# A four-stage transformer kernel on one core: Sinkhorn reciprocals in PSUM, other PSUM pairs for M, mix and attention tiles, whole-row subtractions on GpSimd

## The chip, the core and the metric

The kernel runs on one core of a Trainium2 chip. The metric is the device time of one execution, in microseconds (us); lower is better. The engines are named as in the profile: PE is the matmul engine (TensorE), DVE is VectorE, ACT is ScalarE, POOL is GpSimd, SP issues the DMAs. SBUF is the working memory of 128 partitions. PSUM is the accumulator memory: PE writes it, and DVE and ACT read and write it. This kernel uses it as four pairs of banks, PAIR[0] to PAIR[3], each 128 x 1024 f32.

## The reference, cut to what matters

Four blocks are applied to x (2 x 512 rows of 1024), each with a layer norm in front and a residual added behind:

```python
x = x + fake_quant(ln(x)) @ fake_quant(ctx)                    # 1: quantised product
x = x + hyper_connection(ln(x))                                # 2: Sinkhorn mixing of 4 streams
x = x + attention(ln(x), ctx, Wq, bq, Wk, bk)                  # 3: softmax(Q K^T / 32) @ ctx
x = x + lora_ffn(ln(x), gate, up, down)                        # 4: silu(gate) * up, hidden 2752
```

Block 2 needs, for every row, a 4 x 4 matrix that is normalised 50 times by rows and by columns:

```python
for _ in range(50):
    u = -logsumexp(Z + v[None, :], axis=-1)
    v = -logsumexp(Z + u[:, None], axis=-2)
H_res = exp(Z + u[:, None] + v[None, :])
x_mixed = einsum("tij,tjc->tic", (1 - g) * I + g * H_res, x_streams)
```

## The kernel before

Everything is scheduled by hand: each engine has one program in a fixed order, and engines meet in semaphores. The 1024 rows are eight tiles g = 0..7 of 128 rows; tiles 0 to 3 are batch 0, tiles 4 to 7 batch 1. Matmuls are done in f16 with a high and a low part, so that each product is three matmuls of 128 x 512 (`mm3`, L1894 to L1896). The lower parts are formed by subtracting the high part from the f32 value, on DVE, on ACT or on POOL.

**Sinkhorn.** DVE keeps the 4 x 4 matrices in linear form in SBUF. One step (`sinkhorn_step`, L1285) is three instructions, each waiting for the one before: a sum (L1290), a reciprocal (L1291, into RR, which lies in SBUF) and a product (L1292) of the matrix with the reciprocal, repeated over rows or columns. There are 99 steps for each batch. The first 30 (`JOINT`) are done for both batches at once, on 128 x 128 elements; then the matrices are copied apart (L1300) and 69 steps run on batch 0 alone (128 x 64 elements). The other batch's 69 steps (`second_steps`) come later, in pieces of 1, 27, 11, 11, 11, 6 and 2 between other DVE work: after each of the first pieces DVE takes the lower parts of two projected tiles (`projected_lo`, L1373), then the first score maximum (`maximum`, L1386).

**What runs beside the first Sinkhorn.** PE computes M = Wq^T Wk in eight tiles of two halves (`m_half`), each followed by the subtraction of its high part (`m_rest`, L2061), while ACT takes the high and the low part out of PSUM (L677, L681). M tiles go through three pairs in turn. Between them PE and ACT compute the branch product of block 2 through PAIR[3], and POOL adds its streams (L513 to L516) and adds the result to X (`add_share`, L521).

**After the first Sinkhorn.** `mix_factors` (L1311) gives the factors. Tiles 0 and 1 are mixed by DVE (L1338) and ACT (`mix_help`, L743). For tiles 2 and 3 ACT makes diagonal matrices (`mix_diag`, L755) and PE multiplies (`mix_product`, L2091) into PAIR[0] and PAIR[2]. Tiles 0 to 3 are then normalised (L760), transposed on PE (`third_transpose`, L2108), reduced by their high parts (`third_rest`, L2116) and projected (`project(0, n)`, n = 0..3, one call being 96 matmuls into one pair of PAIR[0] and PAIR[1]). The scores (`score(g)`) and attended tiles (`attend(g)`) follow in the same two pairs, managed by the class `Banks`; a second `Banks` object, `aux`, hands PAIR[2] and PAIR[3] in turn to the constant product, the transposed softmax weights (`weights_transpose`, L1976, read by ACT L821 and DVE L1398) and later transposes.

**The second Sinkhorn** runs on DVE beside `project(0, n)` and `score(0)`; it ends with `mix_factors(1)`, after which DVE mixes tiles 4 to 7 alone. Beside it POOL adds the shares of tiles 4 to 7 and takes the lower parts of context rows (`context_lo`, L531; DVE has its own, L1381). POOL does each row of 1024 in four instructions of 256. A context row's lower part also releases its staging slot to the next DMA.

The order of PE's program around the change is:

```python
mix_product(2); mix_product(3); m_rest(KD - 1)
for g in range(0, BT, 2):
    third_transpose(g); third_transpose(g + 1); third_rest(g); third_rest(g + 1)
```

Of the kernel before, what the change touches and what calls it, by code (L numbers as in the profile page):

```python
# [99 lines left out]
class Banks:  # L100
# [3 lines left out]
    def __init__(self, pairs, uses):  # L104
        self.pairs = pairs
        self.uses = uses
        self.place = {use[0]: i for i, use in enumerate(uses)}

    def pair(self, *name):
        return self.pairs[self.place[name] % len(self.pairs)]  # L110

    def wait_empty(self, eng, *name):
        before = self.place[name] - len(self.pairs)
        if before >= 0:
            eng.wait_ge(self.uses[before][1], self.uses[before][2])


def build(nc, x, ctx, ctx_t, consts, small_w, w_branch, wq, wk, bqk, gate_w, gate_tail, up_w,
          up_tail, down_w, down_tail, gate_a, gate_bt, up_a, up_bt, down_a, down_bt, out_t, x_keep):
    stack = ExitStack()  # L120
    with stack:
# [98 lines left out]
        MIX_PAIR = (None, None, 0, 2)  # L220
# [23 lines left out]
        def factors_of(g, si, sj):  # L244
# [72 lines left out]
            [(("ctk", 0), ctk_ok, 1)]  # L317
            + [(("at", g), at_lo, g + 1) for g in range(BT)]
# [14 lines left out]
        M_PAIR = (2, 1, 0, 2, 1, 0, 2, 1)  # L333
        T3_PAIR = (1, 3, 0, 2)
# [141 lines left out]
        def _(e):  # L476
# [47 lines left out]
            def context_lo(i):  # L524
                n, kind, b, k = context_item(i)
                tile = (CN if kind else CTT)[b][k]
# [3 lines left out]
                for q in range(0, D, CST):  # L530
                    last = e.tensor_tensor(tile[:, 1, q:q + CST], STAGE[n % SLOTS][:, q:q + CST], tile[:, 0, q:q + CST],  # L531
                                           ALU.subtract)
                last.then_inc(c_lo, 1)
# [630 lines left out]
        def _(e):  # L1164
# [119 lines left out]

            def sinkhorn_step(n, z, rs, rr):  # L1285
# [8 lines left out]
            def part(b):  # L1294

                return ZE[:, b * NE:(b + 1) * NE], RS[:, b * n32 // B:(b + 1) * n32 // B], RR[:, b * n32 // B:(b + 1) * n32 // B]
# [357 lines left out]
            for n in range(JOINT):  # L1654
                sinkhorn_step(n, ZP, RS, RR)
# [235 lines left out]
        def _(e):  # L1891
# [132 lines left out]
            def m_half(i, h):  # L2024

                if i == 0 and h == 0:
                    e.wait_ge(w_lo, 2 * KD)
                    e.wait_ge(ht_ok, 7)
                elif i == 1 and h == 0:
                    e.wait_ge(ht_ok, 8)  # L2030
                elif i == 2 and h == 0:
                    e.wait_ge(ctx_ok, 1)
                elif h == 0:
                    e.wait_ge(m_lo, i - 2)
# [49 lines left out]
            def mix_product(g):  # L2084

                dst = PAIR[MIX_PAIR[g]]
                e.wait_ge(m_lo, KD - 4 + g)
# [8 lines left out]
            def third_transpose(g):  # L2096
                e.wait_ge(n3_ok, g + 1)
                if g == 0:
                    e.wait_ge(m_lo, KD)
                elif g == 1:  # L2100
                    e.wait_ge(y_ok, NT)
                    e.wait_ge(braw_ok, 1)
                if g >= BT:
# [62 lines left out]
            def weights_transpose(g):  # L2166
                e.wait_ge(e_ok, g + 1)
# [199 lines left out]
            mix_product(2)  # L2367
            mix_product(3)
            m_rest(KD - 1)
# [137 lines left out]
```

## Time and profile before

| | |
|---|---|
| median of three runs | 1239.46 us (1236.49 to 1240.28) |
| the profiled execution | 1237.51 us, its span 1235.7 us |
| PE busy | 1169.7 us, 95% of the span |
| DVE busy | 797.1 us, 65% |
| ACT busy | 479.5 us, 39% |
| POOL busy | 128.9 us, 10% |

The profile is of one execution. The page gives busy time per engine, the span in 40 slices, and the chain of work that ended last. Other views list who waited for whom, busy time and granted PE clock in chosen stretches, and single instructions in order of time. PE's clock is given as a share of 2.4 GHz, so 0.50 is 1.2 GHz. A DVE instruction's duration includes whatever it waits for after it has started.

### The profile page before, as it was taken

To read this page: it belongs to the slowest core of one execution; us is meant where nothing else is said; L and a number is where in the kernel's file an instruction comes from. 1 tells how busy PE (TensorE), PEld (TensorE's weight loads), DVE (VectorE), ACT (ScalarE), POOL (GpSimd) and SP (SyncE) were. 2 spreads that over 40 slices of the span, in tenths; PEclk is the share of its full clock that TensorE was granted. 3 is DMA by queue.
4 is the path that set the end of the run, shared out by engine and by line. 5 is a ranking of instruction groups with operands and counts; after the bars stand their busy time and mean duration, and the time that the engine had idled before them with its cause. 6 is when DMAs were issued, how large, how long until landed. Compare 5 with 4: busy or idle time off the path is not lost.

```text
span 1235.7 us, 16385 instructions
## 1 busy us (share of the span) xinstructions
PE 1169.7 (95%) x6357; PEld 579.0 (47%) x6362; DVE 797.1 (65%) x1571; ACT 479.5 (39%) x716; POOL 128.9 (10%) x176
## 2 busy tenths in 40 slices
PE   3899999689999999999999999999999999999998
PEld 2345554454444445454444444444444444444444
DVE  6695898989997156887776776767767652222220
ACT  7782851574135124534434434334343231111110
POOL 4410260028002210020000000000001000000000
PEclk9989999899999999999999999999999999999999
DMA  9530000015012114220121121111111231111310
GB/s 370 208 115 1 1 1 1 0 69 152 19 36 100 49 35 139 69 101 24 46 69 68 36 69 44 59 69 34 69 52 24 71 136 46 46 47 46 119 38 26
DMA packets 26062, 83.58 MB, mean 68 GB/s; under 512 B 3648, under 2 KB 4288, under 8 KB 25984
## 3 DMA queue, kind: packets, MB, share of 16 engines
q1 hardware_dynamic: 25984, 82.53, 19.6%
q8 instruction: 51, 0.84, 0.3%
q14 instruction: 27, 0.22, 0.1%
HBM read 76.22 MB, written 6.29 MB: 67 GB/s over the span
## 4 chain that ended last, share of the span: by engine, by line
PE 75%; DVE 17%; ACT 5%; issue 2%; DMA 1%; ACTq 0%; SPq 0%; DVEq 0%
PE PAIR L2257 31%; PE PAIR L1894 11%; PE PAIR L1895 11%; PE PAIR L1896 11%; DVE LORA L1292 3%; DVE LORA L1291 3%; DVE LORA L1290 3%; DVE X L1338 2%; PE PAIR L1959 2%; PE PAIR L2214 2%; PE PAIR L1976 1%; PE PAIR L2091 1%; PE PAIR L1967 1%; PE PAIR L2269 1%; ACT POOL L617 1%
## 5 line engine op out<-in xcount | busy, mean ns | idle before, releaser
L1894 PE MATMUL PAIR<-POOL 128*128 128x512 f16 x688 | 261.3, 380 | 4.8 <-DVE POOL L1381 2.8
L1896 PE MATMUL PAIR<-POOL 128*128 128x512 f16 x688 | 261.3, 380 | 0.0
L1895 PE MATMUL PAIR<-POOL 128*128 128x512 f16 x688 | 261.3, 380 | 0.0
L2257 PE MATMUL PAIR<-XT,POOL 128*128 128x512 f16 (+1 forms) x1056 | 239.0, 379 | 1.0 <-ACT ST L867 1.0
L2257 PEld LDWEIGHTS PAIR<-XT,POOL 128*128 128x128 f16 (+1 forms) x1056 | 102.6, 98 | 120.5 <-issue 2.5
L2257 PE MATMUL PAIR<-X,POOL 128*128 128x512 f16 (+1 forms) x528 | 121.2, 379 | 0.0
L1896 PEld LDWEIGHTS PAIR<-POOL 128*128 128x128 f16 x688 | 67.2, 98 | 81.8 <-issue 0.6
L1894 PEld LDWEIGHTS PAIR<-POOL 128*128 128x128 f16 x688 | 67.1, 98 | 76.6 <-issue 5.5
L1895 PEld LDWEIGHTS PAIR<-POOL 128*128 128x128 f16 x688 | 67.2, 98 | 64.5 <-issue 0.8
L1509 DVE SCALAR_TENSOR_TENSOR STG<-STG,PAIR 128x1024 f32<-128x1024 f32 (+2 forms) x32 | 28.1, 884 | 92.1 <-PE PAIR L2269 89.1
L901 ACT ACTIVATE POOL<-STG 128x1024 f16<-128x1024 f32 (+2 forms) x32 | 25.0, 788 | 144.9 <-DVE STG L1509 144.9
L2257 PEld LDWEIGHTS PAIR<-X,POOL 128*128 128x128 f16 (+1 forms) x528 | 50.9, 98 | 57.4 <-issue 0.4
L1456 DVE TENSOR_TENSOR POOL<-STG,POOL 128x512 f16<-128x512 f32 (+1 forms) x110 | 72.3, 692 | 0.9 <-ACT POOL L852 0.7
L1292 DVE SCALAR_TENSOR_TENSOR LORA<-LORA 128x64 f32<-128x64 f32 (+1 forms) x168 | 61.3, 365 | 5.8
L852 ACT ACTIVATE POOL<-STG 128x512 f16<-128x512 f32 (+1 forms) x110 | 62.6, 611 | 4.5 <-DVE STG L1436 3.6
L2257 PE MATMUL PAIR<-T4B,POOL 128*128 128x512 f16 (+1 forms) x264 | 60.6, 379 | 1.2 <-DVE ST L1477 0.8
L1471 DVE TENSOR_TENSOR POOL<-POOL,PAIR 128x512 f32<-128x512 f32 (+1 forms) x22 | 15.1, 687 | 70.6 <-PE PAIR L2257 70.6
L852 ACT ACTIVATE POOL<-ST 128x512 f16<-128x512 f32 (+1 forms) x44 | 27.1, 616 | 85.1 <-DVE ST L1451 85.1
L545 POOL MEMSET STG<- 96x1024 f32 (+1 forms) x12 | 10.9, 923 | 463.8 <-DVE POOL L1456 418.8
L1894 PE MATMUL PAIR<-XT,POOL 128*128 128x512 f16 x128 | 49.1, 384 | 3.9 <-DVE POOL L1373 2.7
L1436 DVE SCALAR_TENSOR_TENSOR STG<-STG,PAIR 128x1024 f32<-128x1024 f32 (+1 forms) x44 | 52.3, 1190 | 0.0
L1895 PE MATMUL PAIR<-XT,POOL 128*128 128x512 f16 x128 | 49.3, 385 | 0.0
(281 smaller groups left out, 1717.0 us busy)
## 6 DMA issues: line engine op xcount, KB each, us to landing
STG<-in_gate_w SPq DMA_DIRECT2D x21, 512.0 KB, 3.5
STG<-in_up_w SPq DMA_DIRECT2D x21, 512.0 KB, 4.2
STG<-in_ctx_t SPq DMA_DIRECT2D x16, 512.0 KB, 3.8
STG<-in_ctx SPq DMA_DIRECT2D x16, 512.0 KB, 3.6
STG<-in_down_w SPq DMA_DIRECT2D x16, 512.0 KB, 3.5
POOL<-in_ctx SPq DMA_DIRECT2D x12, 512.0 KB, 11.1
X<-in_x SPq DMA_DIRECT2D x8, 512.0 KB, 9.7
out_t<-X SPq DMA_DIRECT2D x16, 256.0 KB, 2.9
```

The source lines that it names most:

```text
L852: e.activation(block(j, name)[:, 0, :, :], src, ACT.Copy).then_inc(b_hi, 1)
L901: e.activation(DWN[(m + 1) % 2][0:kp, 0, k0:k1, :], st, ACT.Copy).then_inc(d_hi, 1)
L1290: chain(e.tensor_reduce(rs, red(z), AX.X, ALU.add))
L1291: chain(e.reciprocal(rr, rs))
L1292: chain(e.scalar_tensor_tensor(flat(z), over(rr), SINK_SCALE, flat(z), ALU.mult, ALU.mult))
L1436: e.scalar_tensor_tensor(st, st, WS, PAIR[aux.pair("fold", n)][:, 0:KD * width], ALU.mult, ALU.add).then_inc(s_add, 1)
L1456: e.tensor_tensor(blk[:, 1, :, :], block_source(j, name)[0], blk[:, 0, :, :], ALU.subtract).then_inc(b_lo, 1)
L1509: e.scalar_tensor_tensor(st, st, WS, PAIR[aux.pair("dfold", m, i)][0:kp, 0:w_], ALU.mult, ALU.add).then_inc(d_add, 1)
L1894: e.matmul(dst, l_hi, r_hi, start=first, stop=False)
L1895: e.matmul(dst, l_hi, r_lo, start=False, stop=False)
L1896: return e.matmul(dst, l_lo, r_hi, start=False, stop=last)
L2257: i = e.matmul(dst, blk[:, a_, k, :], src[:, b_, k, :], start=(opens and k == 0 and n == 0), stop=(k == KD // 2 - 1 and n == 2), skip_grou ...
```

## The change

1. The Sinkhorn reciprocals go to PSUM, into the first 32 columns of PAIR[2] (16 for a single batch), and the product reads them from there. The other operand and the result stay in SBUF.
2. PAIR[2] is therefore kept free while a Sinkhorn runs. M goes through PAIR[1] and PAIR[0] in turn, so tile i waits for tile i-2 to be taken, where it was i-3. `mix_product(2)` and `(3)` go to PAIR[2] and PAIR[1], the four third transposes to pairs 3, 0, 1, 3, the constant product and the transposed weights 0 to 3 to pairs 3, 3, 3, 2, 3.
3. `weights_transpose(2)` waits for the second Sinkhorn's factors. `m_rest(KD - 1)` moves ahead of `mix_product(3)` on PE.
4. POOL's `context_lo` is one instruction of 1024 columns in place of four of 256.

```diff
-        before = self.place[name] - len(self.pairs)
-        if before >= 0:
-            eng.wait_ge(self.uses[before][1], self.uses[before][2])
+        i = self.place[name]
+        for n in range(i - 1, -1, -1):
+            if self.at[n] == self.at[i]:
+                eng.wait_ge(self.uses[n][1], self.uses[n][2])
+                break
-        MIX_PAIR = (None, None, 0, 2)
+        MIX_PAIR = (None, None, 2, 1)
-            [(("ctk", 0), ctk_ok, 1)]
-            + [(("at", g), at_lo, g + 1) for g in range(BT)]
+            [(("ctk", 0), ctk_ok, 1, 3)]
+            + [(("at", g), at_lo, g + 1, (3, 3, 2, 3)[g]) for g in range(BT)]
-        M_PAIR = (2, 1, 0, 2, 1, 0, 2, 1)
-        T3_PAIR = (1, 3, 0, 2)
+        M_PAIR = (1, 0, 1, 0, 1, 0, 1, 0)
+        T3_PAIR = (3, 0, 1, 3)
             def context_lo(i):                                   # POOL
-                for q in range(0, D, CST):
-                    last = e.tensor_tensor(tile[:, 1, q:q + CST], STAGE[n % SLOTS][:, q:q + CST], tile[:, 0, q:q + CST],
-                                           ALU.subtract)
-                last.then_inc(c_lo, 1)
+                e.tensor_tensor(lo, STAGE[n % SLOTS], hi, ALU.subtract).then_inc(c_lo, 1)
+            RP = PAIR[2][:, 0:n32]
-                return ZE[...], RS[...], RR[:, b * n32 // B:(b + 1) * n32 // B]
+                return ZE[...], RS[...], RP[:, 0:n32 // B]
-                sinkhorn_step(n, ZP, RS, RR)
+                sinkhorn_step(n, ZP, RS, RP)
                 if i == 0 and h == 0:                            # m_half
-                    e.wait_ge(ht_ok, 7)
+                    e.wait_ge(ht_ok, 8)
                 elif i == 1 and h == 0:
-                    e.wait_ge(ht_ok, 8)
-                elif i == 2 and h == 0:
                     e.wait_ge(ctx_ok, 1)
                 elif h == 0:
-                    e.wait_ge(m_lo, i - 2)
+                    e.wait_ge(m_lo, i - 1)
-                e.wait_ge(m_lo, KD - 4 + g)                      # mix_product
+                if g == 3:
+                    e.wait_ge(m_lo, KD - 1)
                 if g == 0:                                       # third_transpose
-                    e.wait_ge(m_lo, KD)
-                elif g == 1:
                     e.wait_ge(y_ok, NT)
                     e.wait_ge(braw_ok, 1)
+                elif g == 1:
+                    e.wait_ge(m_lo, KD)
+                elif g == 3:
+                    e.wait_ge(x3a_lo, 1)
             def weights_transpose(g):
+                if g == 2:
+                    e.wait_ge(hr_ok, 2)
             mix_product(2)
+            m_rest(KD - 1)
             mix_product(3)
-            m_rest(KD - 1)
```

## Rows read from the trace of the kernel before

**Rows 1.** The page: busy time per engine, and the last chain's shares by engine.
```profile
PE 1169.7 (95%) x6357; PEld 579.0 (47%) x6362; DVE 797.1 (65%) x1571; ACT 479.5 (39%) x716; POOL 128.9 (10%) x176
PE 75%; DVE 17%; ACT 5%; issue 2%; DMA 1%; ACTq 0%; SPq 0%; DVEq 0%
```

**Rows 2.** Stretches: us, length, busy PE PEld DVE ACT POOL, PEclk, DMA share, GB/s.
```profile
226.00:236.30 10.30, 0.16 (x4) 0.10 (x2) 9.91 (x24) 8.73 (x22) 0.00 (x0) 0.76 0.00 0
...
302.80:315.30 12.50, 12.22 (x48) 5.05 (x48) 11.26 (x40) 1.95 (x3) 5.05 (x8) 0.86 0.32 102
...
388.00:500.00 112.00, 111.96 (x613) 54.96 (x611) 56.88 (x79) 42.02 (x53) 22.55 (x32) 1.00 0.28 87
```

**Rows 3.** PE's waits from 205 to 560 us: total, times, longest.
```profile
PE PAIR L2091 <- ACT T4B L755: 10.1, 1, 10.1
PE PAIR L1894 <- DVE POOL L1373: 4.6, 3, 2.7
PE PAIR L1894 <- DVE POOL L1381: 2.8, 3, 1.8
PE PAIR L2108 <- ACT POOL L760: 2.4, 1, 2.4
...
PE PAIR L1976 <- ACT POOL L760: 1.0, 1, 1.0
```

**Rows 4.** Sinkhorn's product, L1292, by stretch: length, DVE busy (count), PEclk, DMA.
```profile
128.00:166.50 38.50, 14.50 (x30) 1.00 0.00 1
166.50:187.00 20.50, 7.81 (x21) 1.00 0.00 1
187.00:227.30 40.30, 11.01 (x49) 1.00 0.00 1
...
268.50:309.00 40.50, 19.45 (x31) 0.96 0.38 117
```

**Rows 5.** Timeline, 284 to 304 us, POOL and DVE: start, duration of all.
```profile
285.24 15.13 POOL L531 TENSOR_TENSOR POOL<-STG,POOL 128x256 f16<-128x256 f32 x24
...
287.29 1.29 DVE L1373 TENSOR_TENSOR POOL<-PAIR,POOL 128x512 f16<-128x512 f32 x2
```

**Rows 6.** POOL's group L361 by form, and DVE's timeline beside it, 524 to 532.
```profile
L361 POOL TENSOR_TENSOR POOL<-POOL 128x512 f32<-128x512 f32 x1 | 1.5, 1503 | 63.9 <-ACT POOL L827 63.9
...
525.51 3.25 DVE L1456 TENSOR_TENSOR POOL<-STG,POOL 128x512 f16<-128x512 f32 x2
```

**Rows 7.** DVE groups by form: busy us, mean ns of one, idle before.
```profile
L1483 DVE SCALAR_TENSOR_TENSOR POOL<-POOL 128x512 f32<-128x512 f32 x21 | 14.4, 685 | 0.1
...
L1491 DVE SCALAR_TENSOR_TENSOR PAIR<-PAIR,POOL 128x512 f32<-128x512 f32 x21 | 14.6, 696 | 0.0
...
L1179 DVE TENSOR_TENSOR SM<-SM 128x4 f32<-128x4 f32 x4 | 0.7, 163 | 0.1
...
L1366 DVE TENSOR_TENSOR SM<-PAIR,SM 128x4 f32<-128x4 f32 x2 | 0.3, 161 | 0.1
...
L1212 DVE TENSOR_SCALAR SM<-PAIR,SM 128x8 f32<-128x8 f32 x1 | 0.3, 285 | 0.0
L1213 DVE TENSOR_SCALAR SM<-SM 128x8 f32<-128x8 f32 x1 | 0.2, 230 | 0.0
```

**Rows 8.** ACT's timeline, 186 to 270 us: M's parts and the mixing help.
```profile
209.03 1.02 ACT L681 ACTIVATE POOL<-PAIR 128x1024 f16<-128x1024 f32 x1 [5.04 <-PE PAIR L2061]
214.56 1.02 ACT L677 ACTIVATE POOL<-PAIR 128x1024 f16<-128x1024 f32 x1 [4.51 <-PE PAIR L1896]
227.57 6.50 ACT L743 ACTIVATE STG<-POOL,HR 128x256 f32<-128x256 f32 x16 [11.99 <-DVE HR L1311]
...
243.41 1.01 ACT L677 ACTIVATE POOL<-PAIR 128x1024 f16<-128x1024 f32 x1
```

**Rows 9.** Timeline: DVE and PE at the second transposed weights, 326 to 351.
```profile
347.21 1.22 DVE L1398 TENSOR_TENSOR POOL<-PAIR,POOL 128x1024 f16<-128x1024 f32 x1
...
349.14 1.04 PE L1976 MATMUL PAIR<-IDF,XT 128*128 128x128 f32 x8
```

More of the change, by code:

```diff
@@ L104, in __init__ @@
     def __init__(self, pairs, uses):
-        self.pairs = pairs
         self.uses = uses
         self.place = {use[0]: i for i, use in enumerate(uses)}
+        self.at = [use[3] if len(use) > 3 else pairs[i % len(pairs)] for i, use in enumerate(uses)]
     def pair(self, *name):
-        return self.pairs[self.place[name] % len(self.pairs)]
+        return self.at[self.place[name]]
     def wait_empty(self, eng, *name):
-        before = self.place[name] - len(self.pairs)
-        if before >= 0:
-            eng.wait_ge(self.uses[before][1], self.uses[before][2])
+        i = self.place[name]
[3 more added lines that the diff above has]
+                break
 def build(nc, x, ctx, ctx_t, consts, small_w, w_branch, wq, wk, bqk, gate_w, gate_tail, up_w,
@@ L525, in context_lo @@
                 n, kind, b, k = context_item(i)
-                tile = (CN if kind else CTT)[b][k]
+                hi, lo = (((CN if kind else CTT)[b][k])[:, j, :] for j in range(2))
                 if i == 2 * KP:
@@ L1294, in part @@
             def part(b):
-                return ZE[:, b * NE:(b + 1) * NE], RS[:, b * n32 // B:(b + 1) * n32 // B], RR[:, b * n32 // B:(b + 1) * n32 // B]
+                return ZE[:, b * NE:(b + 1) * NE], RS[:, b * n32 // B:(b + 1) * n32 // B], RP[:, 0:n32 // B]
             def take_apart():
```

## The prediction, made before the changed kernel was run

> **What bounds the kernel now.** I read the page first: PE is busy for 95% of the span, but the chain that ended last is 17% DVE [rows 1], so there are stretches in which DVE sets PE's pace. The list of PE's waits says which: 10.1 us in one piece in front of the mixing product, then 4.6 us for DVE's lower parts of the projected tiles, 2.8 us for context rows that DVE subtracts, and 2.4 and 1.0 us for normalised tiles [rows 3]. The busy time by stretch shows the first as a hole (PE busy 0.16 of 10.3 us) and what follows the second as a slow stretch: at a granted clock of 0.86 of 2.4 GHz, 48 matmuls of `project(0, 3)` fill 12.5 us [rows 2]; from 48 x 216 ns, the pace of a matmul at the full clock (start to start in these stretches), it would be 10.4. From 388 to 500 us PE is busy without a hole [rows 2]. So what DVE saves before 388 us counts, and what it saves behind that doesn't.
>
> The last question is what DVE does there. It runs Sinkhorn steps without a pause. The product of a step costs 225 ns from 187 to 227 us (11.01 / 49). In the 21 steps before, it costs 372 ns on average, and from 268.5 to 309 us, 627 ns (19.45 / 31) [rows 4]. What differs is POOL: it is idle in the cheap stretch and runs two-input subtractions or additions in the others, for instance 24 in a row from 285.24 us. In the same row of POOL work two DVE instructions of 128 x 512 that read one operand from PSUM and one from SBUF take 1.29 us together, which is no more than the 0.68 us each that such a size costs elsewhere [rows 5, 7]. So it is the second SBUF operand that makes DVE wait for POOL. The changed product has its second operand in PSUM.
>
> **The change part by part. (a) First Sinkhorn.** The joint steps' products (128 x 128) cost 293 ns each when undisturbed (the median of the 30); 30 of them would be 8.8 us and are 14.50. The 21 of the next stretch would be 4.7 and are 7.81 [rows 4]. That is 5.7 + 3.1 = 8.8 us that goes with the contention. The sum and the reciprocal have one input each and are not stretched.
>
> *What PSUM costs instead.* No row has a short reciprocal that writes PSUM or a product with a repeated PSUM operand, so I bound both. Writing: a product that writes PSUM takes 696 ns where one that writes SBUF takes 685, so +11 ns. Reading: at four elements 161 ns with a PSUM operand against 163 without, so nothing; as the upper end 285 against 230 ns, which is one more scalar operand as well as a PSUM source, so at most +55 ns [rows 7]. I take 0 for the read and +11 for the write, since the first pair is the same operation in one size; below nothing I allow 10 ns. For 99 steps that is 1.1 us, and 8.8 - 1.1 = 7.7 us are left. The ends are 9.8 and 2.3 us.
>
> The Trainium skill says otherwise of the read ("VectorE: DVE Perf Modes", the section on the TRN2 errata): its cycle table charges a VectorE instruction 58 fixed cycles from SBUF and 120 from PSUM. That would be 62 cycles, 65 ns at its 0.96 GHz, on each of the 99 products: an estimate of 6.4 us, which would leave only 1.3 of the 7.7. By that rule this change is nearly worthless for the first Sinkhorn. The pair of rows at four elements doesn't show it.
>
> *Where the 7.7 us go.* ACT has been idle for 11.99 us when the factors come at 227.5, and starts `mix_help` at once [rows 8]. PE stands still for 10.1 us [rows 3]. PE's M tiles end at 226, so 8 us earlier factors still leave PE about 2 us of hole; the whole 7.7 us pass through. Behind it DVE's mixing and ACT's and PE's short stages depend on one another down to `project(0, 0)` at 267.3 us, and all shift by the same amount. PE will have a new small wait: `m_rest(7)` now stands before `mix_product(3)` and needs ACT's high part, which sits at 243.41 us behind a root that waits for DVE [rows 8]; shifted by 7.7 that is 236.7 us. `mix_product(2)` would be done by about 234, so PE waits some 2.7 us, then needs 0.5 and 5.3 us (24 matmuls at 0.22) and is done at 242.2; DVE wants that tile at 250.0 - 7.7 = 242.3. Nothing is lost, unless the clock is low there (up to 2.7 us, as it is before the change, when these matmuls ran at about 0.33). I leave that in the range.
>
> **(b) Second Sinkhorn.** 31 products of 225 ns would be 7.0 us and are 19.45 [rows 4]: 12.5 us less, 0.8 us more for the writes. Counted from the start of `project(0, 0)`, PE needs 4 x 10.4 + 1.6 (constant product) + 10.4 (`score(0)`) = 53.6 us if it never waits, and took 60.2. With steps of 0.83 us DVE delivers the four pairs of lower parts at about 14, 25, 36 and 47 us, before PE needs them (33, at latest 51). So the 4.6 us of waits and the 1.9 us of slow clock go: 6.5 us for PE. DVE reached the second factors at 66.2 us after that start. It now has to wait for `score(0)` at 53.6, then one maximum (1.6) and two steps: 57.3, thus 8.9 us less.
>
> **(c) From there to 388 us** DVE works almost without a pause (mixing, maxima, context rows, norms), and PE waited 2.8 + 1.0 us for it [rows 3]. PE is 6.5 us ahead and has 3.8 us of waits to lose; DVE is 8.9 us ahead. The later of the two decides: 8.9 us. Sum: 7.7 + 8.9 = 16.6 us.
>
> **(d) The edits with no time of their own.** M through two pairs: tile 7 needs tile 5 taken out, done at 210.05, and starts when tile 6 is complete, at 214.5 [rows 8]: 4.5 us of cover, and if ACT's part came later than that, the rest would be added to the M stage. `weights_transpose(1)` now shares a pair with tile 0's and waits for DVE's lower part, done at 348.4; it ran at 349.14 [rows 9], and DVE gains more than PE. Queued behind that wait are `score(3)` and all of attention; without the gain the cover is 0.7 us. `weights_transpose(2)` waits for the second factors, over 20 us early. The third transposes wait for parts of pair 3 that are free before.
>
> **(e) Whole rows on POOL.** Four instructions of about 0.63 us become one of 2.5 us, perhaps 3: one of 512 columns took 1.50 us. In exchange it keeps out any DVE instruction with two SBUF inputs for all of that: beside POOL's 512-column instructions two DVE subtractions took 3.25 us instead of 1.3 [rows 6]. The POOL rows run from 277 to 309 us and from 393 to 409. DVE's work there, apart from the products, is lower parts, attended sums (one PSUM operand each) and statistics (one input). I cost it at nothing; POOL's context rows are ready 10 us before `score(0)` asks for them.
>
> The Trainium skill ("SBUF — State Buffer", who interferes with whom) has the shared port pair held for a whole instruction, so that longer ones on POOL block longer. The 3.25 us agree. It would speak against (e) only if DVE still had such instructions there.
>
> **The rivals.** *Priced reads* (+55 ns, the upper end): (a) gives 2.3 us; steps of 0.89 us make the second factors come at about 59.5, so (b) and (c) give 6.7; together 9 us, 1228.5 to 1230.5. *Slow repeated reads*: if PSUM delivers the repeated operand at half pace, each product costs its elements once more, 67 ns (133 in the joint steps), on top of the 55 and 11: (a) turns into a loss of about 6 us, (b) gives 3, and the time is 1239 to 1242. *The lock stays* (the slower side): if a product with one PSUM operand still waits for POOL, (a) is nothing, and in (b) each of the ten one-row instructions lets one step pass in 2.5 us, where two passed: ten steps late, 8 us, 1245 to 1248. It decides from products of more than about 0.7 us between 268 and 309 us. The two DVE instructions amid POOL's row [rows 5] speak against it. *Given back later*: part of the gain is lost behind 388 us or to a low clock in `mix_product(3)`; 1227 to 1233.
>
> **How the numbers follow.** The profiled execution took 1237.5 us, 2 us below the median of the three; 1237.5 - 16.6 = 1220.9, from the median 1222.9. I take 1221.5 and give it 0.62, priced reads 0.15, given back 0.10, slow reads 0.08, the lock 0.05. The range goes from 1215 (cheaper reads, no slow clock) to 1232, and takes in the priced case. A difference of 0.3%, 3.7 us, is about what can be told from no change. Faster by more: 0.62 + 0.15 + 0.10, less a little for the unnamed, 0.86; within it 0.07; slower 0.07.
>
> **What would show it.** Right: products of 0.22 to 0.30 us with no long ones while POOL works; the hole before L2091 down from 10.1 to about 2.5 us; no waits of L1894 for L1373; `project(0, 0)` at about 259.6. Priced: the undisturbed product at 0.28. The lock: products near 2 us beside L531. Given back: new waits behind 388 us, or 24 mixing matmuls in 8 us.

## The result, and the profile after

The kernel after the change takes 1220.7 us (median of four runs, 1218.3 to 1226.7), the kernel before beside it 1238.3. The ratio is 0.9865 with a 95% interval of 0.9825 to 0.9905. The forecast was 1221.5, in a range of 1215 to 1232. A second set of runs gave 1221.4 against 1239.3, ratio 0.9861 (0.9838 to 0.9884).

The profiled execution of after is the slowest of its four (1226.7 us, span 1224.8); the one of the second set, called *after again* below, has a span of 1220.9. The comparison is made stage by stage, so that what such executions differ in for other reasons can be seen. The stages are cut at starts in the timelines: the first reduction of the Sinkhorn steps (S), the first mixing factors (H1), the first matmul of `project(0, 0)` (P), the second factors (H2), the first transposes of `third_transpose(4)` (T), and the end of the span. All in us:

```
                 0-S     S-H1    H1-P    P-H2    H2-T    T-end   span
before          128.41   98.84   40.05   66.19   53.88   848.34  1235.7
after           132.25   90.12   40.22   58.58   53.95   849.68  1224.8
after again     128.19   90.16   40.23   58.60   54.07   849.62  1220.9
forecast          0      -7.7     0      -8.9     0        0     -16.6
after again
 less before    -0.2     -8.7    +0.2    -7.6    +0.2     +1.3   -14.8
```

The 3.8 us by which the first profile starts the Sinkhorn steps late lie ahead of every changed instruction, and after again doesn't have them. The gain sits in the two stages that were named, with 16.3 us between them where 16.6 were forecast.

The page (busy time per engine, and the last chain's shares), as [rows 1]:

```profile
PE 1172.4 (96%) x6362; PEld 579.8 (47%) x6362; DVE 780.7 (64%) x1571; ACT 479.1 (39%) x716; POOL 121.7 (10%) x128
PE 72%; DVE 17%; ACT 6%; issue 2%; POOL 1%; DMA 1%; ACTq 0%; SPq 0%; DVEq 0%
```

DVE has 16 us less work and POOL 7, PE 3 us more. DVE's groups of the Sinkhorn steps by form (line, operation, count, then busy us and mean ns), the product being L1294 now, as in [rows 7]:

```profile
L1293 DVE RECIPROCAL PAIR<-LORA 128x16 f32<-128x16 f32 x138 | 36.0, 261 | 4.8
...
L1294 DVE SCALAR_TENSOR_TENSOR LORA<-PAIR,LORA 128x64 f32<-128x64 f32 x138 | 30.9, 224 | 4.8
L1293 DVE RECIPROCAL PAIR<-LORA 128x32 f32<-128x32 f32 x30 | 10.8, 361 | 1.0
...
L1294 DVE SCALAR_TENSOR_TENSOR LORA<-PAIR,LORA 128x128 f32<-128x128 f32 x30 | 8.7, 291 | 1.0
```

The same line by stretch (us, length, DVE busy, count, then PE's granted clock, DMA share and rate), as [rows 4]:

```profile
132.00:170.00 38.00, 9.94 (x36) 1.00 0.01 2
170.00:187.50 17.50, 4.77 (x22) 1.00 0.00 1
187.50:222.30 34.80, 9.44 (x43) 1.00 0.01 1
262.60:303.00 40.40, 8.29 (x37) 1.00 0.38 108
```

In the last stretch 37 products take 224 ns each (8.29 / 37), beside POOL rows that made them 627 ns before [rows 4]. PE's waits from 205 to 560 us (total, times, longest), as [rows 3]:

```profile
PE PAIR L2061 <- ACT POOL L676: 2.8, 1, 2.8
PE PAIR L2111 <- ACT POOL L759: 2.4, 1, 2.4
PE PAIR L1896 <- DVE POOL L1383: 2.2, 3, 1.0
...
PE PAIR L2092 <- ACT T4B L754: 1.3, 1, 1.3
...
PE PAIR L1978 <- ACT POOL L759: 0.9, 1, 0.9
```

The hole before the mixing product is down from 10.1 to 1.3 us, the 4.6 us for the projected lower parts are gone, and the new wait of `m_rest(7)` (L2061) is there with 2.8 us. The stretches that answer to [rows 2] (length, busy PE PEld DVE ACT POOL, PEclk, DMA share, GB/s):

```profile
222.40:232.30 9.90, 8.59 (x60) 4.58 (x59) 9.65 (x20) 9.61 (x25) 0.00 (x0) 1.00 0.00 0
302.80:315.30 12.50, 12.50 (x59) 5.68 (x58) 11.08 (x44) 3.69 (x5) 0.39 (x1) 1.00 0.21 76
388.00:500.00 112.00, 109.44 (x583) 52.65 (x582) 60.08 (x91) 34.73 (x49) 14.21 (x12) 0.97 0.26 81
```

One thing was not expected. Timeline, 279 to 293 us, POOL and DVE (start, duration of all, instruction):

```profile
279.71 12.56 POOL L532 TENSOR_TENSOR POOL<-STG,POOL 128x1024 f16<-128x1024 f32 x6
```
```profile
287.68 0.16 DVE L1368 TENSOR_TENSOR SM<-PAIR,SM 128x4 f32<-128x4 f32 x1
287.88 4.42 DVE L1369 TENSOR_SCALAR SM<-SM 128x4 f32<-128x4 f32 x1
292.33 0.17 DVE L1370 TENSOR_SCALAR SM<-SM 128x4 f32<-128x4 f32 x1
```

A `tensor_scalar` of `constant_terms` on four elements, 0.23 us before, takes 4.42, and it ends at 292.30 us with the last of POOL's six rows (292.27). It has one input, and both its input and its output lie in SBUF (tile SM). DVE, with the Sinkhorn steps queued behind it, is late by 4.2 us, and the maximum of tile 0 starts 55.4 us after P where the forecast had 53.6.

### The profile page after: what moved, and what is told of

Its sections match the earlier page's. It is cut to its first block, busy times and chain, and to the rows that moved or that the text cites. A ratio compares the mean times of both kernels' runs of the same rounds, so it can differ in the third digit from the quotient of the medians.

```text
span 1224.8 us, 16343 instructions
## 1 busy us (share of the span) xinstructions
PE 1172.4 (96%) x6362; PEld 579.8 (47%) x6362; DVE 780.7 (64%) x1571; ACT 479.1 (39%) x716; POOL 121.7 (10%) x128
## 4 chain that ended last, share of the span: by engine, by line
PE 72%; DVE 17%; ACT 6%; issue 2%; POOL 1%; DMA 1%; ACTq 0%; SPq 0%; DVEq 0%
PE PAIR L2262 32%; PE PAIR L1896 10%; PE PAIR L1898 10%; PE PAIR L1897 10%; DVE PAIR L1293 3%; DVE LORA L1292 3%; DVE LORA L1294 3%; PE PAIR L1961 2%; DVE X L1340 2%; PE PAIR L2219 2%; PE PAIR L1978 1%; PE PAIR L1969 1%; PE PAIR L2274 1%; PE PAIR L2111 1%; PE PAIR L2002 1%
## 5 line engine op out<-in xcount | busy, mean ns | idle before, releaser
L1293 DVE RECIPROCAL PAIR<-LORA 128x16 f32<-128x16 f32 (+1 forms) x168 | 46.8, 279 | 5.8
```

Of the source, the lines that this page charges most:

```text
L1293: chain(e.reciprocal(rr, rs))
```

## Experiments

**1. Quarters again.** After, but POOL subtracts a context row in four pieces:

```diff
...
-                e.tensor_tensor(lo, STAGE[n % SLOTS], hi, ALU.subtract).then_inc(c_lo, 1)
+                for q in range(0, D, CST):
+                    last = e.tensor_tensor(tile[:, 1, q:q + CST], STAGE[n % SLOTS][:, q:q + CST], tile[:, 0, q:q + CST],
+                                           ALU.subtract)
+                last.then_inc(c_lo, 1)
```

> The kernel after, with GpSimd's context rows taken back to four quarters of 256 columns; the reciprocals in PSUM and all moved pairs stay. Theory (what was costed at nothing is wrong): in the trace of after the four-element tensor_scalar of constant_terms lasted 4.42 us at 287.88 beside six whole rows of 2.1 us, because it stands outside of PSUM on both sides. With quarters of 0.63 us it should be let in within about one quarter or two: at most 1.3 us, probably under 0.9. The maximum of tile 0 then starts when score(0) is done, about 53.6 us after project(0,0) in place of 55.4, and the time falls by 1.3 to 1.8 us against after (about 1219 on the scale where after is 1220.7), while GpSimd's six rows take 15 us in place of 12.6. Rival (the stretched instruction has nothing to do with the row's length): it stays at 4 us or more and the time at that of after within 0.5 us. A second rival: the slower GpSimd rows delay the context rows that score(0) asks for, and the time gets longer; rows of before had them ready 10 us early, so nothing is expected from it.

Measured: 1226.0 us, ratio 0.9881 (0.9854 to 0.9908), where a time near 1219 was expected. S to H1 is 90.18 us as in after; P to H2 is 61.99 in place of 58.58. Timeline of this kernel, POOL and DVE:

```profile
278.74 15.15 POOL L533 TENSOR_TENSOR POOL<-STG,POOL 128x256 f16<-128x256 f32 x24
```
```profile
286.09 7.82 DVE L1372 TENSOR_SCALAR SM<-SM 128x4 f32<-128x4 f32 x1
```

The theory was wrong, and not in size only. The instruction isn't let in after the quarter that is running; it waits through about twelve of them, to 293.91 us, and POOL's 24 end at 293.89. With shorter instructions POOL's run lasts 15.15 us in place of 12.56, so the wait got longer. Whole rows, which I had costed at nothing, thus save 3.4 us of this stage in this kernel.

**2. Whole rows alone.** The kernel before with the inverse of that diff, nothing else.

> The kernel before, with whole rows on GpSimd and nothing else changed: part (e) of the change alone. Theory (a DVE product with two SBUF operands is kept out for the whole of a GpSimd instruction): beside the rows of the second Sinkhorn, which now last 2.1 us each, a product waits up to 2.1 us, one step of three instructions passes for each row, so products there have a maximum of 2 us or more in place of 0.86. The six rows and four before them take 10 x 2.1 = 21 us in place of 25, in which 10 steps pass in place of about 20 at 1.26 us; behind them steps cost 0.84. So DVE is late by about (21 + 10 x 0.84) - 25 = 4 us in the second Sinkhorn, and the time is 3 to 6 us above before, 1241 to 1244 where before is 1238.3. Rival (whole rows cost nothing even without the PSUM reciprocals, since less of GpSimd's time is spent in total): products keep a mean of 0.63 us there and the time is that of before within 1 us.

Measured: 1243.5 us (before beside it 1238.8), ratio 1.0035 (1.0022 to 1.0048): slower, inside the 1241 to 1244 expected. P to H2 takes 69.54 us, 3.35 more than before. DVE's products (L1289 here) beside the whole rows:

```profile
286.19 1.47 DVE L1289 SCALAR_TENSOR_TENSOR LORA<-LORA 128x64 f32<-128x64 f32 x1
...
288.23 1.51 DVE L1289 SCALAR_TENSOR_TENSOR LORA<-LORA 128x64 f32<-128x64 f32 x1
```

Between these two a product is started every 2.04 us, which is one step for each row of 2.1 us. Here each product is let in when the row in progress ends. So part (e) by itself costs 4.7 us in the medians and belongs behind the reciprocals' move.

The theory named the mechanism of the products rightly, but not where most of the time goes. The 69 products of the second Sinkhorn take 29.3 us here and 28.0 in before, only 1.3 more, because POOL is also done 3.4 us earlier. The two `tensor_scalar` of `constant_terms` take 3.9 us in place of 0.4, beside POOL's next run, of two rows (305.19 to 309.39 us):

```profile
305.47 1.86 DVE L1364 TENSOR_SCALAR SM<-SM 128x4 f32<-128x4 f32 x1
307.37 2.05 DVE L1365 TENSOR_SCALAR SM<-SM 128x4 f32<-128x4 f32 x1
```

So the time fell into the expected range partly by luck.

**3. Reciprocals in SBUF.** After, with the reciprocals alone undone:

```diff
-                sinkhorn_step(n, ZP, RS, RP)
+                sinkhorn_step(n, ZP, RS, RR)
...
-                return ZE[:, b * NE:(b + 1) * NE], RS[:, b * n32 // B:(b + 1) * n32 // B], RP[:, 0:n32 // B]
+                return ZE[:, b * NE:(b + 1) * NE], RS[:, b * n32 // B:(b + 1) * n32 // B], RR[:, b * n32 // B:(b + 1) * n32 // B]
```

> The kernel after, with the reciprocals of the Sinkhorn steps written to SBUF again; the moved pairs, the new order of m_rest and mix_product and the whole rows stay. Theory (all of the gain hangs on the product's second operand being in PSUM, the moves are worth nothing): the products of the first Sinkhorn are stretched again (means of about 0.48 and 0.37 us beside GpSimd's 512- and 256-column work in place of 0.30 and 0.22), the first Sinkhorn costs 98 to 99 us in place of 90.1, the wait before the mixing product is 9 to 10 us again, and in the second Sinkhorn products beside whole rows last up to 2.1 us. The time is that of before plus what the whole rows cost: 1238 to 1244. Rival (the moves of M, mix and scores gave part of it): a time of 1226 to 1234 with stretched products all the same.

Measured: 1242.3 us, ratio 1.0024 (1.0011 to 1.0037). S to H1 98.86 us (before 98.84), P to H2 69.46 (experiment 2: 69.54). PE's waits, and the product's group from 270.6 to 313 us:

```profile
PE PAIR L2092 <- ACT T4B L754: 10.1, 1, 10.1
PE PAIR L1896 <- DVE POOL L1375: 7.7, 4, 3.0
```
```profile
L1294 DVE SCALAR_TENSOR_TENSOR LORA<-LORA 128x64 f32<-128x64 f32 x31 | 21.7, 700 | 1.1
```

All the gain of the two stages is in the second operand of the product. The moves of M, mix, scores and attended tiles change no stage by a measurable amount; what they do is make room for it. From H1 to P it takes 39.14 us (before 40.05); what the new order of `m_rest(7)` does there is shown by experiment 6.

**4. The constant's terms in PSUM.** After, with the intermediate results kept out of SBUF:

```diff
-                chain(e.tensor_tensor(cb, cp[:, :, 1], cb, ALU.add))
-                chain(e.tensor_scalar(cb, cb, 1.0 / WS, col(C0), ALU.mult, ALU.add))
-                e.tensor_scalar(cb, cb, 1.0 / 32.0, None, ALU.mult).then_inc(ctk_ok, 1)
+                chain(e.tensor_tensor(cp[:, :, 1], cp[:, :, 1], cb, ALU.add))
+                chain(e.tensor_scalar(cp[:, :, 0], cp[:, :, 1], 1.0 / WS, col(C0), ALU.mult, ALU.add))
+                e.tensor_scalar(cb, cp[:, :, 0], 1.0 / 32.0, None, ALU.mult).then_inc(ctk_ok, 1)
```

> The kernel after, with the intermediate results of constant_terms kept in PSUM, so that no tensor_scalar there has both its input and its output in SBUF; four instructions on 4 elements as before, whole rows on GpSimd as in after. Theory (a DVE instruction waits for GpSimd when it stands in SBUF on both sides, also with one input and four elements, and one side in PSUM frees it): the instruction that took 4.42 us takes 0.2 to 0.3 us, DVE has its 4.2 us back, the maximum of tile 0 starts 53.6 to 54 us after project(0,0) in place of 55.4, and the time falls by 1.3 to 1.8 us against after (about 1219 where after is 1220.7). Rival (4.42 us was the wait for the scalar operand of the constant or something else in SBUF that stays there): the same instruction still takes over 2 us, or the next one does, and the time stays.

Measured: 1219.8 us, ratio 0.9844 (0.9821 to 0.9867). DVE's timeline there:

```profile
283.74 0.17 DVE L1368 TENSOR_TENSOR PAIR<-PAIR,SM 128x4 f32<-128x4 f32 x1
283.94 0.23 DVE L1369 TENSOR_SCALAR PAIR<-PAIR,SM 128x4 f32<-128x4 f32 x1
284.20 0.16 DVE L1370 TENSOR_SCALAR SM<-PAIR 128x4 f32<-128x4 f32 x1
```

The 4.42 us are 0.23, although the scalar operand is still in SBUF; the maximum of tile 0 starts 53.7 us after P, and P to H2 is 56.85 us, 1.73 less than after, where the forecast had 57.3. So it was that input and output stood in SBUF, and behind it `score(0)` decides, as forecast.

**5. Once more, beside after.** After and the kernel of experiment 4 in one set on another chip.

> The kernel after, unchanged, as the control for the other kernels of this call: 0.985 to 0.989 of before, 1220 to 1225 us. If its profiled execution has the start of the first Sinkhorn step at 128 us (before had 128.4, the first profile of after 132.3), the span should be about 1221, since the 3.8 us lay ahead of every changed instruction. The four-element tensor_scalar of constant_terms should again end together with the last of the six whole rows on GpSimd, after 4 us or more.

> The kernel after with the intermediate results of constant_terms in PSUM, once more beside after on the same chip, as the candidate for a better kernel. From the profiles: 1.8 us less from the first to the second mixing factors (97.0 against 98.8) and DVE 4.2 us ahead behind them, where DVE sets the pace until 388 us, so 2 to 4 us faster than after: 1218 to 1220 where after is 1222. Rival: DVE's 4.2 us are given back at the next wait of DVE for PE (score, attended sums), and the difference stays under 1 us.

Measured: after 1221.4 us (0.9861), the other 1219.6 (0.9852, 0.9830 to 0.9874). P to H2 is 58.60 and again 56.85. Both medians of the new kernel are 1 to 2 us lower, and the stage says 1.7, but the intervals overlap, so by the runs' times alone they are not told apart. The 2 to 4 us that were expected of DVE's 4.2 us are not there: the maximum waits for `score(0)`, which ends 53.6 us after P, and of DVE's lead 1.7 us are left. The expected start at 128 us held for after again (128.19), and it shows that the start is not the kernel's: it was 131.02 for the other, and over all profiles of this study it lies between 128.0 and 132.6.

This pair shows another thing. From H1 to P after took 40.2 us in both profiles and experiment 4's kernel 40.16 in its first, but 37.52 in its second, with the same waits of PE. PE's third transposes of tiles 2 and 3, first in after, then in experiment 4's kernel the second time:

```profile
253.10 6.54 PE L2111 MATMUL PAIR<-IDF,POOL 128*128 128x128 f32 x32 [2.42 <-ACT POOL L759]
```
```profile
251.91 3.84 PE L2111 MATMUL PAIR<-IDF,POOL 128*128 128x128 f32 x32 [2.42 <-ACT POOL L759]
```

The stretch from 250 to 260 us of the two, in the same order (the third number from the end is the granted clock):

```profile
250.00:260.00 10.00, 7.51 (x48) 7.25 (x48) 8.55 (x38) 5.52 (x8) 0.00 (x0) 0.66 0.33 134
```
```profile
250.00:260.00 10.00, 6.21 (x54) 5.15 (x55) 8.77 (x37) 8.22 (x11) 0.00 (x0) 1.00 0.23 94
```

That is 2.7 us, present or not from one execution to the next of one kernel, behind the same wait of 2.42 us. In after PE is granted 1.2 GHz from 251.97 to 258.80 us, over nearly all of these transposes, and in the other 2.4 GHz throughout.

**6. The old order of `m_rest(7)`**, on the kernel of experiment 4:

```diff
             mix_product(2)
-            m_rest(KD - 1)
             mix_product(3)
+            m_rest(KD - 1)
```

> The same with m_rest(7) behind mix_product(3) again, as in the kernel before. Theory: the 2.8 us for which PE waits in m_rest(7) for ACT's high part lie beside DVE's work (DVE waited only 0.39 us for the mixing product of tile 3), so mixing product 3 comes 2.8 us earlier and at most 0.4 us reach the path; ACT's lower part of M's last tile then waits for m_rest until 242.7 in place of 241.9 and the normalised tile 1 behind it comes up to 1 us later. Net within 0.7 us of the kernel beside it, of either sign. Rival (PE's new wait costs its 2.8 us): 2 to 3 us faster than the kernel beside it.

Measured: 1220.3 us, ratio 0.9847 (0.9827 to 0.9866), not told apart from the 1219.6 of the kernel beside it. H1 to P takes 37.74 us against 37.52, but the two differ in PE's clock. The third transposes of tiles 2 and 3, in this kernel:

```profile
247.59 5.47 PE L2111 MATMUL PAIR<-IDF,POOL 128*128 128x128 f32 x32 [2.42 <-ACT POOL L759]
```

They take 5.47 us, partly at 1.2 GHz, where the kernel beside it took 3.84 at 2.4 GHz. They start 29.32 us behind H1, in the kernel beside it 30.73. So at one clock the old order is 1.4 us faster, twice the 0.7 expected at most. With the new order DVE waits 0.38 us for tile 3's mixing product and then for ACT's square root, which comes behind the later first transposes; in this kernel neither wait is there. The second wait, in the kernel beside it:

```profile
248.94 0.17 DVE L1177 RECIPROCAL SM<-SM 128x2 f32<-128x2 f32 x1 [1.03 <-ACT SM L598]
```

The new order isn't free, then, but it has a use where the mixing product is slow. In experiments 3 and 7 the first 24 mixing matmuls take 8.0 us, most of it at 1.2 GHz, behind 10 us of standing (5.45 us in this kernel), and the same transposes still start 30.7 us behind H1; in before and experiment 2, with the old order and the same slow matmuls, it is 31.9 and 31.6.

**7. The second Sinkhorn alone.** After, with the reciprocals in SBUF for the joint steps and batch 0:

```diff
-                sinkhorn_step(n, ZP, RS, RP)
+                sinkhorn_step(n, ZP, RS, RR)
...
-                return ZE[:, b * NE:(b + 1) * NE], RS[:, b * n32 // B:(b + 1) * n32 // B], RP[:, 0:n32 // B]
+                return ZE[:, b * NE:(b + 1) * NE], RS[:, b * n32 // B:(b + 1) * n32 // B], RP[:, 0:n32 // B] if b else RR[:, 0:n32 // B]
```

> The kernel after, with the reciprocals in SBUF for the first Sinkhorn (joint steps and batch 0) and in PSUM for batch 1 alone. Theory (the two gains are separate and add up): the first Sinkhorn takes 98.8 us again and PE stands still for 9 to 10 us before the mixing product, so 8.7 us of the gain are gone; from the first to the second factors it takes 98.5 to 99 us as in after (before 106.2). The time is 8 to 9 us above after and 7 to 9 below before: 1229.5 to 1231.5. Rival (the first part's gain is what makes the second possible, or the other way round, because PE gets late beside DVE): 1226 or 1235 and more.

Measured: 1227.4 us, ratio 0.9917 (0.9897 to 0.9937), 2 us under the range. S to H1 is 98.87 us, P to H2 58.56 (after 58.60): the stages are as expected and each gain stands without the other. The product's groups, batch 0 and batch 1:

```profile
L1294 DVE SCALAR_TENSOR_TENSOR LORA<-LORA 128x64 f32<-128x64 f32 x69 | 18.8, 272 | 2.4
L1294 DVE SCALAR_TENSOR_TENSOR LORA<-PAIR,LORA 128x64 f32<-128x64 f32 x69 | 15.5, 224 | 2.4
```

The 2 us come from elsewhere in its profile: H1 to P is 39.14 us, 1.1 less than after again, and T to the end 846.93, 2.7 less. Between two executions of experiment 4's kernel the first varied by 2.6 us (40.16 and 37.52) and the second by 1.2 (846.9 and 848.2); what moves the second is told below, under "Behind T".

**8 and 9. What kind of instruction is kept out?** On experiment 1's kernel and on after, the stalled instruction gets a second input in place of being a `tensor_scalar`:

```diff
-                chain(e.tensor_scalar(cb, cb, 1.0 / WS, col(C0), ALU.mult, ALU.add))
+                chain(e.scalar_tensor_tensor(cb, cb, 1.0 / WS, col(C0).to_broadcast([P, BT]), ALU.mult, ALU.add))
```

> After with quarters on GpSimd (as in the first experiment), and the third of the four instructions of constant_terms written with two inputs of 4 elements in SBUF (scalar_tensor_tensor with the constant's column repeated) in place of one (tensor_scalar); the fourth stays a tensor_scalar. Theory (it is the kind of instruction: one with two inputs is let in between two of GpSimd's back-to-back instructions, as the Sinkhorn products of before were, at most 0.86 us; a tensor_scalar from SBUF to SBUF is let in only when GpSimd's whole run of instructions pauses): the third takes at most 0.9 us and the fourth takes over the wait, 6 to 7.5 us, ending together with GpSimd's run of 24; the time is that of the first experiment, 1222 to 1226. Rival (it is the place in time or the chip's arbitration of that moment): the third takes several us again, or both are short and the time falls to 1219 to 1221.

> After itself (whole rows on GpSimd), with the same edit to the third instruction of constant_terms. Theory: with two inputs it is let in at the next end of a row, so it takes at most 2.1 us plus its own 0.2; the fourth, a tensor_scalar, waits from there to the end of the six rows, and both end where the 4.42 us ended. Rival: it waits over 2.5 us.

Measured, POOL and DVE, first with quarters (1223.2 us), then with whole rows (1219.8 us, one run each):

```profile
276.52 15.15 POOL L533 TENSOR_TENSOR POOL<-STG,POOL 128x256 f16<-128x256 f32 x24
```
```profile
285.07 6.61 DVE L1372 SCALAR_TENSOR_TENSOR SM<-SM 128x4 f32<-128x4 f32 x1
```
```profile
275.74 12.59 POOL L532 TENSOR_TENSOR POOL<-STG,POOL 128x1024 f16<-128x1024 f32 x6
```
```profile
285.18 3.17 DVE L1369 SCALAR_TENSOR_TENSOR SM<-SM 128x4 f32<-128x4 f32 x1
```

Both end with POOL's run (291.68 and 291.67; 288.35 and 288.33). The theory falls: two inputs wait for the whole run as one input does.

**10. A product of the old form in that place.** On experiment 1's kernel, two instructions more in front of the `tensor_scalar`; the first writes batch 0's matrix, which is dead by then:

```diff
+                if b == 0:
+                    z0 = part(0)[0]
+                    chain(e.scalar_tensor_tensor(flat_column(z0), over_column(RR[:, 0:n32 // B]), 1.0, flat_column(z0),
+                                                 ALU.mult, ALU.mult))
+                    chain(e.scalar_tensor_tensor(z0[:, 0:BT], RR[:, 0:BT], 1.0, z0[:, 0:BT], ALU.mult, ALU.mult))
```

> The kernel of the first experiment (after, quarters on GpSimd) with two instructions put in front of the tensor_scalar of constant_terms(0) that took 7.82 us there: first one in the form of the old Sinkhorn product, two inputs of 64 elements in SBUF, on batch 0's matrix, which nobody reads any more; then the same operation on 4 elements of the same tile. What is open is why the products of before were let in between two GpSimd instructions (0.86 us at most) while the 4-element instructions beside the same 24 GpSimd instructions waited for the last of them (7.82 us with one input, 6.61 us with two). Theory A (size decides): the first takes 0.2 to 0.9 us, the second takes 5 to 7 us and ends with GpSimd's last, the tensor_scalar is short. Theory B (operands decide: the tile SM or the column as scalar operand): the first and the second take 0.2 to 0.9 us each, the tensor_scalar 4 to 6 us. Theory C (the moment decides: after a two-input DVE instruction of 512 columns, or with no DVE instruction of this kind ahead of it in GpSimd's run): the first takes 6 us or more, the others are short. In all three the sum is about that of the first experiment, and the time 1222 to 1227.

Measured (1227.5 us, one run), POOL and then DVE:

```profile
280.13 15.14 POOL L533 TENSOR_TENSOR POOL<-STG,POOL 128x256 f16<-128x256 f32 x24
```
```profile
287.48 7.87 DVE L1374 SCALAR_TENSOR_TENSOR LORA<-LORA 128x64 f32<-128x64 f32 x1
295.39 0.16 DVE L1376 SCALAR_TENSOR_TENSOR LORA<-LORA 128x4 f32<-128x4 f32 x1
295.58 0.23 DVE L1377 TENSOR_SCALAR SM<-SM 128x4 f32<-128x4 f32 x1
```

This is what theory C expects: neither size nor tile nor operation decides, but the moment. The form that took 0.80 us at most beside these rows in before takes 7.87 here. What is different about the moment is open.

One pattern holds in every profile I have. Take POOL's work in unbroken runs, and of each run the first DVE instruction whose operands all lie in SBUF (those that only reduce, or take reciprocals, were never stretched and don't count). Where that first one asked within 1 us of the start of the run, it and all that followed were let in at the end of one POOL instruction. In before it stood 0.08 us behind the start of the run from 269.27 to 300.37 us, and 22 more followed, 0.80 us at most. Where the first one came 23.3 to 24.6 us after the start, it waited for the end of the run: after, after again and experiments 1, 7, 8, 9 and 10. Experiment 2 has the very `tensor_scalar` 0.28 us behind the start of a run of two rows, and it is let in when the first of them ends (1.86 us). Whether this is the cause was not tried: it is a pattern, and the cause stays open.

**11. Quarters on the better kernel.** Experiment 4's kernel with experiment 1's diff.

> The kernel with the intermediate results of constant_terms in PSUM, and quarters on GpSimd in place of whole rows. Theory (once no DVE instruction beside GpSimd's rows has all its operands in SBUF, the length of GpSimd's instructions costs DVE nothing, and GpSimd itself has cover): project(0,0) to the second mixing factors takes 56.85 us as in its counterpart with whole rows, no wait of DVE or PE is new, and the time is within 0.2% of 1219.6. Rival (the shorter instructions are worth something by themselves, or their 15 us in place of 12.6 are late for score(0)): a difference of over 2 us, seen as a changed wait of score(0)'s matmuls.

Measured: 1218.8 us, ratio 0.9838 (0.9818 to 0.9857). P to H2 is 56.85 us to the hundredth. Once no product and no `tensor_scalar` of DVE beside POOL's rows stands in SBUF with all its operands (the sums do, and were never stretched), the length of POOL's instructions is worth nothing, as the prediction's part (e) had it under that very condition.

The kernels of experiments 4, 6 and 11 are the fastest here, 1218.8 to 1220.3 us, all faster than before by their intervals; against after (1220.7 and 1221.4) the 1.7 us are seen in the stage P to H2 and not resolved in the times.

## Why the prediction was right, point by point

**(a) First Sinkhorn: 7.7 us forecast, 8.7 measured.** The 99 products fell from 33.3 to 24.2 us, 9.1 (8.8 were forecast); the price of writing to PSUM is 8 ns (253 to 261, 353 to 361), 0.8 us for 99 where 1.1 was taken; reading costs nothing, 224 ns against the 225 of undisturbed ones. The two copies of `take_apart` were not in the sum: in before they ran at 166.59 us in a run of POOL's (162.09 to 167.13) and took 0.70 us, in after they run at 164.87, 1 us ahead of one, and take 0.30. Together that is 9.1 - 0.8 + 0.4 = 8.7 us.

The Trainium skill ("VectorE: DVE Perf Modes", the section on the TRN2 errata) charges PSUM sources 62 cycles more, which by the prediction's estimate would have left 1.3 us. The measurement decides: 224 ns with the operand in PSUM, and the same at four elements (162 against 160 to 163 ns).

**The passage from H1 to P**, forecast to shift as a whole, took 40.2 us in place of 40.05, but not because nothing in it changed. The wait of `m_rest(7)` was put at 2.7 us and is 2.8; "nothing is lost" by it is wrong, since experiment 6 puts the new order at 1.4 us. The rival of a slow clock didn't come in `mix_product`, which ran at full pace, and the third transposes lost 2.7 us instead. Before had lost some 2.5 us of this passage at its first mixing product (8.04 us against 5.45), which came behind 10.1 us of standing, and 1.4 at the transposes (5.24 against 3.84). Without these terms each is 36.1 us long: 40.05 - 2.5 - 1.4, and 40.2 - 2.7 - 1.4. That the stage came out as forecast is luck. `project(0, 0)` was forecast for 259.6 us and starts at 258.6 in after again.

**(b) Second Sinkhorn: 8.9 forecast, 7.6 measured.** This is the step that failed, and the fault is in (e): "I cost it at nothing". I listed DVE's work beside POOL's rows as PSUM operands and one-input statistics and overlooked the two `tensor_scalar` of `constant_terms`, SBUF on both sides. In before they ran at 303.09 and 303.36 us, just ahead of POOL's next run at 303.69, so these two showed no trouble; once DVE came faster the first of them fell into POOL's run. The trace of before did hold a sign that instructions with one input can be stretched too, the copies of `take_apart` amid POOL's work:

```profile
166.59 0.70 DVE L1300 COPY LORA<-LORA 128x64 f32<-128x64 f32 x2
```

Two of them take 0.30 us in after. The price of the stall is 4.2 us of DVE, of which 1.7 reach H2 (58.60 - 56.85). Without it the stage is 56.85, 9.3 less than before. PE's part of the sum was right: `score(0)` ends 53.6 us after P. (One call of `project` is 48 matmuls, as the prediction counts, and not the 96 of the section on the kernel before.)

The Trainium skill ("SBUF — State Buffer", who interferes with whom) names `tensor_scalar` among the instructions that can take the shared pair; I had read from it only what it says of two inputs. Experiments 1 and 4 agree that it takes part. The page has the loser wait for one instruction; the 7.82 and 7.87 us are some twelve of POOL's.

**(c) DVE decides from 333 to 388 us.** H2 to T is 53.9 to 54.1 us in before, after, and experiments 1 and 3, however early H2 comes: the gain of DVE passes on whole, and PE still has its waits for context rows (2.2 us, was 2.8).

**Behind T** I forecast nothing and 1.3 us are given back. PE's waits there are as before; the stretch from 480 to 510 us, after and then the second profile of experiment 4's kernel:

```profile
480.00:510.00 30.00, 27.44 (x143) 14.03 (x141) 25.49 (x42) 16.51 (x21) 0.00 (x0) 0.89 0.21 71
```
```profile
480.00:510.00 30.00, 27.43 (x153) 14.83 (x152) 27.15 (x47) 15.53 (x21) 2.91 (x2) 0.94 0.22 78
```

PE stands for the same 2.6 us in both, and in before, which had 0.94 too; 0.05 of 30 us is 1.5 us of PE's pace. All fourteen profiles of this study order themselves by this clock. Over the stretch from 478 to 518 us PE stands 2.6 us in each of them; the granted clock is 1.00 in seven, and these end 846.9 us behind T; it is 0.96 in five, before among them, and these end 848.1 to 848.3 us behind T; it is 0.91 in both profiles of after, with 849.6 and 849.7. The kernel of experiment 9, which differs from after in one short instruction, has 1.00 and 846.9. So the 1.3 us are a difference in granted clock, which varied between the two executions of experiment 4's kernel as well (1.00 and 0.96); that both profiles of after had the lowest value is most likely chance, but with two profiles this isn't shown.

**(d) The covers held.** ACT takes out M's tile 5 at 212.88 us and tile 6 is complete at 218.41, the 4.5 us that were counted; `weights_transpose(1)` runs 1.5 us after DVE's lower part is done (cover 0.7 before). Experiment 3 puts the moves at nothing, and experiment 6 the order of `m_rest(7)` at 1.4 us. **(e)** A whole row takes 2.1 us, not 2.5 to 3; the rest is told under (b).

**The lock as a rival** described another kernel: "each one-row instruction lets one step pass" is what experiments 2 and 3 show, where the operand is in SBUF. Its price of 8 us was too high: the 69 products took 1.3 and 3.5 us more there than in before.

The sum, 16.6, stands against 17.6 and 17.9 us between the medians and 14.8 between two profiles. Executions differ by more than that gap, and (a) and (b) missed in opposite directions, so the close hit of 1221.5 is in part luck. The mechanism, DVE's products freed from POOL and both gains passed on whole, was right.

## What to carry to other kernels

When a short DVE operation sits beside POOL work, put one of its two inputs into PSUM: the write costs 8 ns, the read nothing, and in none of these profiles was such a product kept out. Then list every other DVE instruction that can fall beside POOL's runs once DVE is faster, also those with one input and four elements, and look at where they stood by luck in the trace of before. Change the length of POOL's instructions only after that: alone it cost 4.7 us, with one straggler left it saved 3.4 in its stage, and with none it is worth nothing. And where two executions differ by 1 to 3 us, look at PE's granted clock stage by stage before a cause is sought in the change: here it hid a loss of 1.4 us.

## What the runs showed of the hardware

- A DVE instruction with input and output in SBUF can wait for the end of POOL's whole unbroken run (4.42 us through two and a fraction rows, 7.82 and 7.87 us through about twelve quarters), not for the instruction in progress; in other moments such an instruction is let in at the end of the POOL instruction in progress (a product took 0.86 us at most beside 256 columns, 2.20 beside whole rows). Input and output in PSUM free it (0.23 us), with the scalar operand left in SBUF.
- One subtraction of 128 x 1024 on POOL takes 2.1 us, four of 128 x 256 take 2.5.
- A copy of 128 x 64 from SBUF to SBUF, one input, took 0.60 us amid POOL's additions and 0.20 without.
- Sums and reciprocals of the Sinkhorn steps, one input, SBUF to SBUF, were not stretched beside the same POOL work (the 138 reciprocals of 128 x 16 in before all took 253 or 254 ns).
- A short reciprocal that writes PSUM takes 8 ns more than one that writes SBUF. A product reads its repeated operand from PSUM as fast as from SBUF (224 and 225 ns).
- The same 32 transposes behind the same 2.42 us of standing took 3.84 or 6.54 us, in two executions of kernels that don't differ there: at 2.4 GHz, and at 1.2 GHz but for the last of them (granted clock 1.00 and 0.66 from 250 to 260 us).
- Behind 10 us of standing PE's next 24 matmuls took 7.8 to 8.0 us, most of it at 1.2 GHz, in all four kernels that have this wait; behind 1.3 to 1.4 us of standing they took 5.45 in all others.
